# One layer of gated cross-attention and routed experts: the projections of the attention spread in halves between the scores, GpSimd's work held behind the maxima, two buffers for a group's sums

## The reference

```python
def _L0_xattn_ref(query, key, value, Wq, bq, Wk, bk, Wv, bv, Wo, bo):
    Q, K, V = proj(query, Wq, bq), proj(key, Wk, bk), proj(value, Wv, bv)   # 16 heads of 32
    scores = jnp.einsum('bhqd,bhkd->bhqk', Q, K) / SCALE
    attn = jax.nn.softmax(scores, axis=-1)
    out = jnp.einsum('bhqk,bhkd->bhqd', attn, V)
    ...
    return out @ Wo.T + bo
...
x = x + jnp.tanh(g_xattn[0]) * _L0_xattn_ref(_layernorm(x, axis=-1), ctx_1024, ctx_1024, ...)
x = x + jnp.tanh(g_ffn[0]) * _L0_ffn_ref(_layernorm(x, axis=-1), ...)   # softmax router, top 2, capacity
return x
```

## Time and profile before

| | |
|---|---|
| median of three runs | 1959.58 us |
| the profiled execution itself | 1961.34 us |
| its span, first to last instruction | 1959.6 us |
| mean granted clock of TensorE | 0.964 |
| busy: PE, DVE, ACT, POOL | 1788.7, 1167.3, 780.9, 484.3 us |
| one batch in the middle: stretch and PE busy | 117.50 and 113.65 us |
| 1110 to 1960 us (experts): PE busy | 832.46 of 850 us |

### The profile page before, as it was taken

One profiled execution on the slowest core, in us unless ns is written; L12 is line 12 of the kernel. 1 busy time (PEld: TensorE's weight loads), 2 busy tenths in 40 slices (PEclk: granted clock), 3 DMA queues, 4 the chain that ended last, 5 costly groups with the idle time before them and its releaser, 6 DMA issues.

```text
span 1959.6 us, 30460 instructions
## 1 busy us (share of the span) xinstructions
PE 1788.7 (91%) x10822; PEld 919.9 (47%) x10822; DVE 1167.3 (60%) x2163; ACT 780.9 (40%) x1012; POOL 484.3 (25%) x451
## 2 busy tenths in 40 slices
PE   7999999999999999999811799999999999999996
PEld 4334242332424334242200566667676767666664
DVE  5777868777686777867587453635354443534330
ACT  5443634445354443634430342515161524334240
POOL 2313333232333313331141121221212211112101
PEclk9999999999999999999955899999999999999998
DMA  6214123150322414023130153433334342424311
GB/s 223 84 44 151 45 94 100 48 166 22 127 66 82 133 43 153 19 73 100 37 141 1 48 141 72 149 77 121 102 96 124 82 140 50 154 66 138 70 45 25
DMA packets 138205, 178.97 MB, mean 91 GB/s; under 512 B 45492, under 2 KB 86592, under 8 KB 134056
## 3 DMA queue, kind: packets, MB, share of 16 engines
q1 hardware_dynamic: 97192, 157.85, 24.7%
q0 software_dynamic: 40960, 20.41, 6.0%
HBM read 134.08 MB, written 43.63 MB: 91 GB/s over the span
## 4 chain that ended last, share of the span: by engine, by line
PE 83%; DVE 9%; ACT 3%; issue 2%; DMA 2%; SPq 1%; POOL 1%; DVEq 0%; ACTq 0%; POOLq 0%
PE psum L1445 21%; PE psum L1422 20%; PE psum L1158 7%; PE psum L1255 6%; PE psum L1262 6%; PE psum L1246 5%; PE psum L1236 5%; PE psum L1335 4%; PE psum L1273 4%; DVE mx L831 2%; PE psum L1163 2%; ACT osum L717 1%; DMA qk_rows<-qks 1%; PE psum L1398 1%; DVE cmp L980 1%
## 5 line engine op out<-in xcount | busy, mean ns | idle before, releaser
L1445 PE MATMUL psum<-w,hT 128*123 128x512 f16 x1920 | 420.3, 379 | 0.0
L831 DVE TENSOR_REDUCE mx<-psum 128x1 f32<-128x512 f32 x512 | 328.5, 684 | 153.4 <-PE psum L1236 152.6
L1422 PE MATMUL psum<-xgT,w 128*128 128x308 f16 (+1 forms) x3072 | 411.3, 294 | 0.6 <-DVE xgT L1089 0.6
L1422 PEld LDWEIGHTS psum<-xgT,w 128*128 128x128 f16 x3072 | 298.4, 97 | 109.7 <-DVE xgT L1089 0.8
L1445 PEld LDWEIGHTS psum<-w,hT 128*123 128x123 f16 x1920 | 257.9, 135 | 148.8
L709 ACT ACTIVATE pt<-psum 128x1024 f32<-128x1024 f32 x256 | 259.3, 1022 | 171.0 <-PE psum L1246 171.0
L759 ACT ACTIVATE h<-psum,b1c 128x308 f32<-128x308 f32 (+1 forms) x256 | 118.1, 512 | 379.4 <-PE psum L1422 379.0
L1107 DVE TENSOR_TENSOR hT<-h,hT 128x615 f16<-128x615 f32 x128 | 102.6, 801 | 212.2 <-ACT hT L762 212.1
L629 POOL DMA_INDIRECT out_dram<-y,idx_now x40 | 98.9, 2473 | 499.6 <-DVE y L1142 273.9
L1236 PE MATMUL psum<-stk 96*128 96x512 f16 x512 | 171.7, 384 | 20.0 <-DVE mx L831 18.9
L1158 PE MATMUL psum<-actT,wT 128*128 128x512 f16 x768 | 168.6, 381 | 2.0 <-DVE wT L818 2.0
(11 more groups left out here) (181 smaller groups left out, 1682.1 us busy)
## 6 DMA issues: line engine op xcount, KB each, us to landing
stage<-in_L_ffn_W_dram SPq DMA_DIRECT2D x64, 1024.0 KB, 5.0
stk<-qk_rows SPq DMA_DIRECT2D x192, 128.0 KB, 2.5
qk_rows<-qks SPq DMA_DIRECT2D x64, 256.0 KB, 2.6
xin<-in_x_dram SPq DMA_DIRECT2D x8, 1024.0 KB, 5.1
cin<-in_ctx_dram SPq DMA_DIRECT2D x8, 1024.0 KB, 5.1
xres<-in_x_dram SPq DMA_DIRECT2D x8, 1024.0 KB, 5.8
out_dram<-xres SPq DMA_DIRECT2D x32, 256.0 KB, 2.1
x_split<-x2hl SPq DMA_DIRECT2D x32, 256.0 KB, 2.3
```

The lines of the kernel that those rows point to most:

```text
L831: v.reduce_max(mx[:, KT * t + qt:KT * t + qt + 1], ps, AX.X).then_inc(read, 1)
L1422: mm = t_.matmul(psum[:, (2 * m + ch) % 4, 0:c1 - c0], w1[:, wp, kt, m * P:(m + 1) * P], xgT[:, xp, kt, c0:c1], start=(kt == 0 and (wp, xp ...
L1445: mm = t_.matmul(psum[0:CP, Y_BANK[c], :], hT[:, hp, k, c * CP:(c + 1) * CP], w2[:, wp, k, :], start=(k == 0 and (hp, wp) == (0, 0)), stop ...
```

## The change

- Ahead of slot 0 stand only four projections and the values' first two; projections 4 to 7 follow in slots 0, 1, 3 and 4, values 2 and 3 in slots 5 and 6, each in two halves: one between the second and third score, one at the slot's end (`filling`). The transposes of slot 2 go in halves too, `parts` goes to the end of slot 4, `logits` to that of slot 5. The banks change with them: the four transposes have four banks (6, 7, 3, 5), the values 3, 5, 3, 6, the logits 6 and 7.
- VectorE takes the first two maxima of a slot ahead of the turn, the statistics of the next input in slots 1 to 4, and the reciprocals at the slots of `RECIP_SLOT` (the first group's norm in slot 14 instead of 13).
- `osum` has two buffers.
- GpSimd does the inverse deviations of the second norm in the next batch, two ahead of the first projection's difference and two ahead of the third's; it waits for the first turn before projection 6, for the second before it norms the input, for the third before it touches `xres`. The input is normed in place (`xn` is `xin`), so SyncE loads the next one at the batch's start, with the context.
- SyncE stacks projections 6 and 7 behind the first group's maxima; stores and the load of `xres` go behind the second's.

```diff
-LN_SLOT = LAG_B
-V_HALF = ((0, 0), (1, 1), (3, 3), (4, 5))
-X2T_SLOT, LG_SLOT = 2, 4
+LN_SLOT = 1
+QK_FIRST, QK_SLOT = 4, (0, 1, 3, 4)
+V_FIRST, V_SLOT = 2, (5, 6)
+X2T_SLOT, PARTS_SLOT, LG_SLOT = 2, 4, 5
+STORE_GROUP = 1
-GROUP_NORM = [t + 3 if t < UNITS else min(t + 2, SLOTS) for t in GROUP_END]
+RECIP_SLOT = ((11, 12, 13, 14), (15, 16, 16, 17), (19, 19, 20, 20), (23, 23, 23, 23))
+GROUP_NORM = [slots[-1] for slots in RECIP_SLOT]
...
-        xn = sb("xn", [P, KT, D], f32)
+        xn = xin
-        osum = sb("osum", [P, 2, S], f32)
+        osum = sb("osum", [P, 2, 2, S], f32)
...
@@ SyncE, batch
-                    sp.wait_ge(xn_ready, KT * b + KT)
+                    sp.wait_ge(act_hi, 2 * KT * b + 2 * KT)
                     sp.dma_start(xin[:, :, :], x_b[b + 1]).then_inc(x_in, 16)
-                    sp.wait_ge(act_hi, 2 * KT * b + 2 * KT)
                     sp.dma_start(cin[:, :, :], c_b[b + 1]).then_inc(c_in, 16)
-                for i in range(NQ):
+                for i in range(QK_FIRST + 2):
                     stack_heads(sp, b, i)
...
                     if g == 0:
+                        for i in range(QK_FIRST + 2, NQ):
+                            stack_heads(sp, b, i)
+                    if g == STORE_GROUP:
                         if not first:
                             store_rows(b)
@@ GpSimd, batch
                 for i, (which, m) in enumerate(QK_ORDER):
+                    if i in (0, 2) and not first:
+                        for tt in (i, i + 1):
+                            inverse_deviation(1, tt, KT * b + (tt - KT))
+                    if i == QK_FIRST + 2:
+                        pool.wait_ge(mrow_ready, NG * b + 1)
...
+                pool.wait_ge(mrow_ready, NG * b + 2)
                 if not last:
...
+                pool.wait_ge(mrow_ready, NG * b + 3)
                 pool.wait_ge(xres_in, 16 * b + 16)
...
-                for tt in range(KT):
-                    inverse_deviation(1, tt, KT * b + tt)
@@ ScalarE, batch
-                        act.wait_ge(norm_done, NG * b + gr)
-                        s.activation(osum[:, :, :], psum[:, 6:8, :], ACT.Copy).then_inc(osum_ready, 1)
+                        act.wait_ge(norm_done, NG * b + max(gr - 1, 0))
+                        s.activation(osum[:, gr % 2, :, :], psum[:, 6:8, :], ACT.Copy).then_inc(osum_ready, 1)
@@ VectorE, batch
                 for t in range(SLOTS + 1):
+                    maxima(t, (0, 1))
                     if t % 4 == 0 and 4 <= t <= UNITS:
...
-                    maxima(t, range(KT))
+                    maxima(t, (2, 3))
...
-                            if t == min(GROUP_END[g] + max(quarter, 1), GROUP_NORM[g]):
+                            if t == RECIP_SLOT[g][quarter]:
                                 reciprocals(g, (quarter,))
@@ TensorE, batch
+                def filling(s, half):
+                    for i in later_qk(s):
+                        queries_keys(i, (half,))
+                    if s == X2T_SLOT:
+                        rows((2 * half, 2 * half + 1))
+                    if (s, half) == (PARTS_SLOT, 1):
+                        parts()
+                    for tt in later_v(s):
+                        values(tt, (half,))
+                    if (s, half) == (LG_SLOT, 1):
+                        logits()
+                for i in range(QK_FIRST):
+                    queries_keys(i)
+                for tt in range(V_FIRST):
+                    values(tt)
...
                     scores(s, 0)
                     scores(s, 1)
-                    if s == X2T_SLOT:
-                        rows()
-                    for tt in range(KT):
-                        if s in V_HALF[tt]:
-                            values(tt, V_HALF[tt].index(s))
-                    if s == LG_SLOT:
-                        parts()
+                    filling(s, 0)
...
                     scores(s, 2)
                     less_maxima(u, 1)
                     scores(s, 3)
-                    for tt in range(KT):
-                        if V_HALF[tt] == (s, s):
-                            values(tt, 1)
-                    if s == LG_SLOT:
-                        logits()
                     with_ones(s - LAG_C)
+                    filling(s, 1)
```

More of the change, by code:

```diff
@@ L663, in _ @@
                         inputs_hi(n, kt)
-            act.wait_ge(bias_ready, 2)
+            act.wait_ge(bias_ready, 1)
+            copied(act, pre, "bias")
             def router_copy(where, b, slot):
@@ L678, in logits, with queries_keys @@
                     s.activation(lg[:, slot, :], ps[:, 0:KT * E], ACT.Copy).then_inc(read, 1)
-                return rows, logits
+                return rows, parts, logits
             def batch(b, last):
-                rows, logits = router_copy(use, b, b)
-                heads_stacked(act, b)
-                for i, (which, m) in enumerate(QK_ORDER):
+                rows, parts, logits = router_copy(use, b, b)
+                def queries_keys(i):
+                    which, m = QK_ORDER[i]
                     n = "qk".index(which)
@@ L710, in batch @@
                                          scale=1.0 / (math.sqrt(HD) * SQ * SQ)).then_inc(read, 1)
+                    if t >= LAG_B:
+                        for tt in later_v(t):
+                            values(tt)
                     if t in GROUP_END[:-1]:
@@ L726, in _ @@
             batch(B - 1, True)
-            rows, logits = router_copy(post, 0, B)
+            rows, parts, logits = router_copy(post, 0, B)
             rows()
+            parts()
             logits()
@@ L1193, in router, with rows @@
             def router(where, b, n):
-                def rows():
+                def rows(kts=range(KT)):
                     pe.wait_ge(x2n_ready, n)
-                    for kt in range(KT):
+                    for kt in kts:
                         dst, full = claim(pe, where, ("x2T", kt), b)
@@ L1222, in batch, with queries_keys @@
                 rows, parts, logits = router(use, b, KT * b)
-                for i, (which, m) in enumerate(QK_ORDER):
+                def queries_keys(i, halves=range(2)):
+                    which, m = QK_ORDER[i]
                     n = "qk".index(which)
@@ L1227, in batch @@
                             copied(pe, act_use, ("actT", n, kt), b)
-                    dst, full = claim(pe, use, ("qk", i), b)
-                    product(dst, [(wT[:, n, wp, kt, m * P:(m + 1) * P], actT[:, n, xp, kt, :])
-                                  for kt in range(KT) for wp, xp in PARTS]).then_inc(full, 1)
+                    if 0 in halves:
+                        claim(pe, use, ("qk", i), b)
+                    bank, _ = use(("qk", i), b)
+                    for kt in [2 * half + j for half in halves for j in range(2)]:
+                        for wp, xp in PARTS:
+                            last = t_.matmul(psum[:, bank, :], wT[:, n, wp, kt, m * P:(m + 1) * P], actT[:, n, xp, kt, :],
+                                             start=(kt == 0 and (wp, xp) == (0, 0)),
+                                             stop=(kt == KT - 1 and (wp, xp) == (1, 0)))
+                    if 1 in halves:
+                        last.then_inc(bank_full[bank], 1)
                 def scores(s, qt):
@@ L1264, in with_ones, with values @@
                         last.then_inc(pv_done, 1)
-                def values(tt, half):
-                    if half == 0:
+                def values(tt, halves=range(2)):
+                    if 0 in halves:
                         claim(pe, use, ("v", tt), b)
                     bank, _ = use(("v", tt), b)
-                    for kt in (2 * half, 2 * half + 1):
+                    for kt in [2 * half + j for half in halves for j in range(2)]:
                         for xp, wp in PARTS:
```

75 lines of the change are left out of this document (51 added, 24 removed).

## The result

Five runs of the changed kernel took 1926.61 to 1928.57 us, 1927.96 in the median, against 1959.58 (five runs, 1956.11 to 1960.03) before: the ratio is 0.9842, 95% interval 0.9829 to 0.9856, a gain of 31.6 us. The forecast was 1940, a gain of 19.6, with a range down to 1931.

What follows compares the result with a forecast made beforehand. TensorE's instructions were taken as the floor, so only its holes could be won: 3.42 us removed less 1.35 added, -2.07 in each of batches 1 to 6, with -2.3 and -4.9 at the ends, -19.6 in total: 1940 us, range 1933 to 1949.

Steps and rivals of the forecast that it cites:

- Removed, per batch: TensorE's holes in slots 2 to 6, 11 and 12 that the change closes: 3.42 us a batch.
- 31 us at the very most: Ceiling of the gain: holes of about 3.9 us in each of eight batches on TensorE.
- The added terms: New costs per batch at slot 0's start, slots 1 to 4, slot 16 and slot 7: 1.35 us in sum.
- (a): Start of slot 0: stacked heads ready in time, VectorE's late split rows stall TensorE by 0.2 us a batch.
- (b): Slots 1 to 4: the next input's statistics load VectorE and stall TensorE, 0.8 us a batch, bounds 0.3 and 1.5.
- (c): Slot 16: two reciprocals instead of one delay the second group's norm and the sums' copy at slot 18, 0.25 us.
- (d): Slot 7: the last values, copied at the end of slot 6, are waited for by 0.1 us.
- The two ends: Batch 0 gains 2.3 us; batch 7 gains 4.9 us, with its DMA wait and low clock gone.
- The first: Rival: slot 0's entry, waiting for stacked heads or VectorE, gives back everything and more, about 1968 us; chance 0.10.
- The second: Rival: VectorE's debts, 2.85 us a batch, cancel the gain, about 1952 to 1957 us; chance 0.13.
- The third: Rival: small holes in slots 0 to 3 lower TensorE's clock, 1.5 us on 7 batches, 1950 us; chance 0.05.
- the fourth: Rival: the change does less than it says; second buffer and holds touch nothing late, already in the sum; no chance given.

Runs made afterwards that it cites:

- a1: Changed kernel with the statistics of the next input in slots 4 to 7 instead of 1 to 4; 1923.25 us, period 112.80.
- a5: Changed kernel with the inverse deviations of tiles 2 and 3 ahead of the second difference instead of the third; 1926.79 us, period 113.22.
- b1: Kernel before with VectorE's part alone: first two maxima ahead of the turn, one reciprocal a slot, two buffers for sums; 1950.45 us, period 116.68.
- b2: Changed kernel without VectorE's part: four maxima behind the turn, two reciprocals in one slot, one buffer for sums; 1936.12 us, period 114.80.
- c1: Kernel before with the router's parts ahead of the half value product in slot 4; 1955.62 us against 1959.87, period 116.77.
- a4: Changed kernel with the second norm's four inverse deviations at the end of their batch again; 1941.14 us, periods 115.08 to 115.58, last looped batch 117.17.
- a2: Changed kernel with one buffer for a group's sums, reciprocals still one a slot; 1937.73 us, period 114.80.
- a3: Changed kernel without GpSimd's three waits for the turns; 1936.54 us, periods of 114.64 to 114.95.
- a6: Changed kernel with GpSimd held only ahead of the residual's bias, the first two holds left out; 1927.20 us, period 113.68.
- f3: Changed kernel with statistics in slots 4 to 7, two later deviations ahead of the second difference, and the copy of sums in two; 1914.93 us.

## Why the prediction missed

**The step that failed is the size of "Removed, per batch".** It summed 3.42 us of brackets and of one stretched pair. Read by the starts of the same rows the holes are 0.41, 0.74 and 0.38 in slot 2 (two of them in the earlier trace rows with 0.57 and 0.21), 0.43 and 0.45 on the values' and the logits' copy, 0.74, 0.37 and 0.73 in slots 5 to 7, 0.62 in slot 12: 4.87 a batch. The stretched pair at 426.72 and the 0.26 behind it, 0.56 in the prediction, are one hole of 0.73. Less the 1.25 added that is 3.62 of the 3.87 measured. The last 0.25 is three gaps of before that are gone after: 0.10 in the second eight transposes (410.90 to 411.88, 0.98 for 0.88), 0.07 behind the logits (421.03 to 421.91, 0.88 for 0.81), and the 0.08 of slot 14. So the removed term was 5.1 us and not 3.42, and nothing is left over for another cause; a1, a5, b1 and b2 each give by their own starts what their periods show (0.69 for 0.72, 0.31 for 0.30, 0.70 for 0.70, 1.26 for 1.28).

**"31 us at the very most"** failed for the same reason: 117.5 - 113.65 counts the overlapping ends of matmuls as busy. The traces' difference is 33.4.

**The added terms held.** (a) 0.2 forecast, 0.31 measured; VectorE's release was met within 0.1 us, by two errors that cancel (above), and the stacked heads were in time. (b) 0.8 forecast, 0.27 + 0.37 + 0.30 = 0.94, of which 0.25 isn't due to the statistics (a1); and the 2.05 that it took for slot 2's transposes held holes, as they take 1.76 without any. (c) 0.25 forecast, nothing found: the hole of slot 19 is what it was. (d) 0.1 forecast, nothing. Sum 1.35 forecast, 1.25 measured: the sum fits better than its terms, as (a) and (b) were set too low and (c) and (d) too high.

**The two ends.** Batch 7 lost 7.02 instead of 4.9, mostly by the same undercount: its DMA wait is 1.10 by the starts (894.94 to 896.26, 1.32 for 0.22) where the bracket has 0.93, and each of its other holes was as short in the sum as in the looped batches. By the starts 5.99 us of holes were removed, and 1.38 for the low clock (898.52 to 901.65, 3.13 where the looped batch takes 1.75); less 0.31 added that is 7.06.

```profile
894.94 0.39 PE L1236 MATMUL psum<-stk 96*128 96x512 f16 x1 [0.21 <-DVE mx L831]
```

The changed kernel has neither that wait nor the stretch of low clock:

```profile
864.00:872.00 8.00, 8.00 (x47) 2.67 (x48) 4.95 (x9) 4.60 (x6) 0.00 (x0) 1.00 0.19 57
```

But these 7.02 are not the change's alone. c1, whose swap is worth 0.61 in a looped batch, lost 2.43 in this one: its wait there is 0.50, and the clock stayed at 1.00. b1 lost 3.18 with neither wait nor fall, though all eight stackings stand ahead of the maxima's DMA in both. So the reason given for the wait, SyncE's eight stackings, isn't enough by itself. The traces show a slower last store: its loads follow it after 4.47 us in the kernel before (886.78 to 891.25), after 2.78 in c1 and 2.54 in b1; why is open. At the other end a hole of 1.99 or 2.00 stands at 28 to 29 us in all fifteen traces. Before and after both show a clock of 0.91 over 20 to 40 us behind it, so the -3.25 is a fair comparison; b1, in which the clock stayed at 1.00, gained there by that too.

**The rivals.** The first did not happen; a4 shows that its wait for the stacked heads would have come, had the deviations stayed, and that its fall of the clock would have been rare (one batch of seven). The second did not: VectorE's debts came to 1.25 a batch where it needed 2.85. The third did not: the clock is at 1.00 from 40 to 930 us of the changed kernel. In the fourth I called the second buffer and the holds idle; a2 and a3 show them worth 1.28 and 1.4 us a batch, as covers for the change's own moves (the later norm, the residual's bias that falls on the turn of slot 12). The forecast was not hurt by it, since both were in place, but its reason was wrong: 20 us of slack was counted for the wait, and the port that they keep free was not looked at.

## What to carry to other kernels

Measure a hole in a pipelined engine from start to start, against the same pair of instructions where nothing waits, and never by the idle time that stands behind a modelled end: here the brackets and one stretched pair held 3.4 of 5.1 us, and holes of 0.3 had no bracket at all. When every engine has slack on average, deal the filler out so that the engine which must answer has its time between any two questions. A step that looks idle in such a change may be the cover of another: take it away alone before calling it so.

## What was not expected of the hardware

The same hole of TensorE left its granted clock at 1.00 in one run and not in another. The one of 1.99 or 2.00 at 28 to 29 us was followed by 0.91 over 20 to 40 us in nine traces, before and after among them, and by 1.00 in six (a2, a3, a4, a6, b1, f3). In a4 a hole of 2.10 was followed by 0.72 over 6 us, and one of 2.20 by 1.00. In the kernel before 0.93 behind two smaller ones was followed by 0.54 over 3.2 us, while in a2 1.46 left the clock at 1.00. The length of a single hole does not tell which it will be.
